# A query stage in less memory, with a fifth context group loaded beside it, in a one-core transformer-block kernel

## What is computed

```
x = x + xattn(layernorm(x), ctx, Wq, bq, Wk, bk, Wv, bv)    # q @ k.T, softmax over 1601, @ v, no scale
x = x + attn(layernorm(x), ...)                             # causal, 16 heads, + exp(denom_bias) in the sum
x = x + ffn(layernorm(x), ...)                              # two mixtures of 64 experts, top 2, gelu between
```

## Time and profile before

| what | value |
|---|---|
| median of 3 runs | 1413.24 us |
| the profiled execution, its own time | 1403.64 us |
| its span, first to last instruction | 1401.8 us |
| PE busy | 1272.8 us, 91% of the span |
| DVE busy | 810.4 us, 58% |
| chain that ended last | PE 75%, DVE 10%, issue 6%, DMA 4% |
| granted TensorE clock, mean | 0.962 |

### The profile page before, as it was taken

The page is one execution under the profiler, slowest core; times in us unless marked ns, Lnnn a source line. Parts: engine busy times, 40 slices in busy tenths (PEclk is TensorE's granted clock), DMA queues, the critical chain, the costliest instruction groups (busy, mean ns, idle before and its releaser), DMA issues.

```text
span 1401.8 us, 61977 instructions
## 1 busy us (share of the span) xinstructions
PE 1272.8 (91%) x27944; PEld 821.5 (59%) x27944; DVE 810.4 (58%) x1511; ACT 442.6 (32%) x927; POOL 207.9 (15%) x364
## 2 busy tenths in 40 slices
PE   7999799999999999999999999578888888798886
PEld 4875233333333335566666666467777777787775
DVE  2435577777767661656556556345473746247666
ACT  0322122122122122222112221136363636336554
POOL 0100000000000000111111111115151523113212
PEclk9999999999999999999999999888999999759999
DMA  8674979989989974311100111212121205522212
GB/s 307 170 226 148 311 250 321 298 278 323 300 278 318 298 252 103 58 60 60 60 37 23 60 45 61 79 43 90 60 109 41 120 0 230 194 90 91 106 45 90
DMA packets 68080, 211.50 MB, mean 151 GB/s; under 512 B 14448, under 2 KB 30832, under 8 KB 53520
## 3 DMA queue, kind: packets, MB, share of 16 engines
q1 hardware_dynamic: 67984, 210.16, 44.5%
HBM read 172.37 MB, written 37.75 MB: 150 GB/s over the span
## 4 chain that ended last, share of the span: by engine, by line
PE 75%; DVE 10%; issue 6%; DMA 4%; ACT 2%; POOL 2%; SPq 1%; DVEq 0%; POOLq 0%; ACTq 0%
PE ps L680 13%; PE ps L529 10%; PE ps L981 8%; PE ps L1756 5%; PE ps L1710 4%; PE ps L233 4%; DVE arena L541 4%; PE ps L437 4%; PE ps L1082 4%; PE ps L1725 3%; PE ps L1742 2%; PE ps L1681 2%; PE ps L670 2%; PE ps L1002 2%; PE ps L1799 2%
## 5 line engine op out<-in xcount | busy, mean ns | idle before, releaser
L541 DVE STREAM_TRANSPOSE arena<-arena 128x448 f32<-128x448 f32 (+1 forms) x512 | 264.2, 577 | 124.7 <-PE ps L529 100.6
L529 PE MATMUL ps<-arena 32*64 32x400 f32 (+1 forms) x4096 | 203.9, 509 | 7.6 <-DVE arena L541 6.9
L680 PE MATMUL ps<-arena 128*64 128x512 f32 x832 | 189.1, 598 | 0.0
L529 PEld LDWEIGHTS ps<-arena 32*64 32x64 f32 x4096 | 75.3, 131 | 104.6 <-DVE arena L541 51.1
L680 PEld LDWEIGHTS ps<-arena 128*64 128x64 f32 x832 | 55.5, 136 | 121.3 <-issue 111.9
L562 ACT ACTIVATE arena<-ps,arena 128x384 f32<-128x384 f32 x64 | 36.4, 583 | 276.3 <-DVE arena L553 276.3
L981 PE MATMUL ps<-arena 128*128 128x256 f32 x512 | 114.8, 382 | 6.4 <-ACT arena L939 6.4
L1596 ACT COPY arena<-ps 128x512 f32<-128x512 f32 x128 | 75.3, 588 | 142.2 <-PE ps L1725 78.5
L981 PEld LDWEIGHTS ps<-arena 128*128 128x128 f32 x512 | 96.0, 190 | 21.2 <-ACT arena L939 7.2
L1416 DVE SCALAR_TENSOR_TENSOR arena<-ps,arena 128x512 f32<-128x512 f32 x64 | 68.8, 1106 | 39.9 <-PE ps L1742 39.6
L1756 PE MATMUL ps<-arena 64*64 64x32 f32 x4096 | 84.5, 236 | 6.5 <-DVE arena L1433 5.8
(11 more groups left out here) (144 smaller groups left out, 1860.3 us busy)
## 6 DMA issues: line engine op xcount, KB each, us to landing
arena<-ctx SPq DMA_DIRECT2D x64, 1024.0 KB
arena<-ctx SPq DMA_DIRECT2D x32, 768.0 KB
arena<-q_n SPq DMA_DIRECT2D x64, 256.0 KB, 11.8
h_n<-arena SPq DMA_DIRECT2D x16, 1024.0 KB, 4.5
arena<-h_n SPq DMA_DIRECT2D x16, 1024.0 KB, 9.8
arena<-x SPq DMA_DIRECT2D x16, 512.0 KB, 4.4
arena<-ctx SPq DMA_DIRECT2D x32, 256.0 KB
x_n<-arena SPq DMA_DIRECT2D x16, 512.0 KB, 3.1
```

Of the source, the lines that this page charges most:

```text
L529: last = pe.matmul(ps[b * SEQ:(b + 1) * SEQ, tb, 0:WIDTH[tb]], qs[p % 2][r, db, b * SEQ:(b + 1) * SEQ], z[r, at % RING, b, 0:WIDTH[tb]], s ...
L541: vec.transpose(z[:, at % RING, :, g * 224:g * 224 + nt * 32].rearrange("p b (j t) -> p b j t", t=32), slots[slot_of(k)][:, :, 0:nt, db * ...
L680: last = pe.matmul(ps[b * SEQ:(b + 1) * SEQ, OB, :], probt[:, j, b * SEQ:(b + 1) * SEQ], slot[:, b, jj, :], start=j == 0, stop=j == TILES - 1)
```

## The change

- `xn` is gone: rows are normalised in place in `xt`. So `load_rows(n)` now waits until tile n-2 has been transposed (`s_t`) and not just normalised.
- The area of slot 2 (group 4) holds only `bq_wide` and `lnt[0]`, both used up early. `xt`, `u_wide` and `parts` move to `spare`; `lnt` of tiles 1 to 7 alternates between two pieces of the zone where wq and wk lay.
- `queries` of tiles 0 to 5 alternate between the two halves of `qs[1]`, the buffer for the queries of odd pairs; tiles 6 and 7 use `xt`. ACT's results of tiles 2 to 5 therefore wait for the store of the tile two before (`s_qd`), and the queries of pair 1 can be loaded only after six stores have landed.
- SP's list is written anew: biases and weights ahead of the first rows, and group 4 in two parts between the stores of tiles 4, 5 and 6. `cross` no longer waits and no longer loads it.
- PE multiplies the first two of the four blocks of wqk before it transposes tile 0.
- POOL's last memset waits for products of tile 6 and not for a store.

```diff
-    queries = [temp(DC, QROWS) for _ in range(4)]
-    queries += [queries[0], queries[1], spare(DC, QROWS), spare(DC, QROWS)]
+    xt = [spare(2 * D) for _ in range(2)]
+    halves_of_qs = qs[1].rearrange("p (u m) q -> p u (m q)", u=2)
+    queries = [t.rearrange("p (c n) -> p c n", c=DC) for t in [halves_of_qs[:, n % 2] for n in range(6)] + xt]
...
+    u_wide = spare(DC, 32)
+    parts = spare(QROWS)
     bq_wide = area(DC, P)
-    xt = [area(2 * D) for _ in range(2)]
-    xn = [area(2 * D) for _ in range(2)]
-    lnt = [area(DC, QROWS) for _ in range(2)]
-    u_wide = area(DC, 32)
-    parts = area(QROWS)
+    own_lnt = [temp(DC, QROWS)]
+    temp.at = temp_at + TILES * P
+    own_lnt.append(temp(DC, QROWS))
+    lnt = [area(DC, QROWS)] + [own_lnt[n % 2] for n in range(1, QUADS)]
...
         def load_rows(n):
             if n >= 2:
-                sp.wait_ge(s_xn, 2 * (n - 2) + 2)
+                sp.wait_ge(s_t, 2 * (n - 2) + 2)
...
-        load_rows(0)
-        load_rows(1)
-        sp.dma_start(wq, a["wq"].rearrange("(c p) d -> p c d", p=P)).then_inc(s_w, 16)
-        sp.dma_start(wk, a["wk"].rearrange("(c p) d -> p c d", p=P)).then_inc(s_w, 16)
         sp.dma_start(bqc, a["bq"]).then_inc(s_b, 16)
         sp.dma_start(bkc, a["bk"]).then_inc(s_b, 16)
+        sp.dma_start(wq, a["wq"].rearrange("(c p) d -> p c d", p=P)).then_inc(s_w, 16)
+        sp.dma_start(wk, a["wk"].rearrange("(c p) d -> p c d", p=P)).then_inc(s_w, 16)
+        load_rows(0)
+        load_rows(1)
         load_context(sp, a, slots, s_c, 0)
-        load_rows(2)
         sp.wait_ge(s_pad, 2)
+        load_rows(2)
         load_context(sp, a, slots, s_c, 1, (0,))
         load_rows(3)
         load_context(sp, a, slots, s_c, 1, (1,))
+        store_queries(0)
         load_rows(4)
-        load_rows(5)
-        store_queries(0)
         load_context(sp, a, slots, s_c, 2, (0,))
-        load_rows(6)
         sp.wait_ge(s_qd, 8 * 16)
         load_queries(sp, a, qs, s_qs, 0)
-        load_queries(sp, a, qs, s_qs, 1)
         store_queries(1)
-        load_rows(7)
+        load_rows(5)
         load_context(sp, a, slots, s_c, 2, (1,))
         store_queries(2)
+        load_rows(6)
         load_context(sp, a, slots, s_c, 3, (0,))
         store_queries(3)
+        load_rows(7)
         load_context(sp, a, slots, s_c, 3, (1,))
-        for n in range(4, QUADS):
-            store_queries(n)
+        store_queries(4)
+        load_context(sp, a, slots, s_c, 4, (0,))
+        store_queries(5)
+        sp.wait_ge(s_qd, 8 * 16 * 6)
+        load_queries(sp, a, qs, s_qs, 1)
+        load_context(sp, a, slots, s_c, 4, (1,))
+        store_queries(6)
+        store_queries(7)
...
-        pool.wait_ge(s_qd, 6 * 8 * 16)
+        pool.wait_ge(s_q, DC * (QUADS - 1))
...
-            if n >= 2:
-                vec.wait_ge(s_t, 2 * (n - 2) + 2)
             for par in range(2):
-                vec.tensor_scalar(xn[u][:, par * D:(par + 1) * D], xt[u][:, par * D:(par + 1) * D],
+                vec.tensor_scalar(xt[u][:, par * D:(par + 1) * D], xt[u][:, par * D:(par + 1) * D],
...
-            if n in (4, 5):
-                act.wait_ge(s_qd, 8 * 16 * (n - 3))
+            if 2 <= n < 6:
+                act.wait_ge(s_qd, 8 * 16 * (n - 1))
...
-        for par in range(2):
-            transposes(0, par)
         pe.wait_ge(s_w, 32)
         pe.wait_ge(s_b, 32)
         for m in range(DC):
+            if m == 2:
+                for par in range(2):
+                    transposes(0, par)
...
-        sp.wait_ge(s_re, 2 * QUADS)
-        load_context(sp, a, slots, s_c, 4)
```

More of the change, by code:

```diff
@@ L284, in store_queries @@
                       .then_inc(s_qd, 16)
+        sp.dma_start(bqc, a["bq"]).then_inc(s_b, 16)
+        sp.dma_start(bkc, a["bk"]).then_inc(s_b, 16)
+        sp.dma_start(wq, a["wq"].rearrange("(c p) d -> p c d", p=P)).then_inc(s_w, 16)
+        sp.dma_start(wk, a["wk"].rearrange("(c p) d -> p c d", p=P)).then_inc(s_w, 16)
         load_rows(0)
         load_rows(1)
-        sp.dma_start(wq, a["wq"].rearrange("(c p) d -> p c d", p=P)).then_inc(s_w, 16)
-        sp.dma_start(wk, a["wk"].rearrange("(c p) d -> p c d", p=P)).then_inc(s_w, 16)
-        sp.dma_start(bqc, a["bq"]).then_inc(s_b, 16)
-        sp.dma_start(bkc, a["bk"]).then_inc(s_b, 16)
         load_context(sp, a, slots, s_c, 0)
+        sp.wait_ge(s_pad, 2)
         load_rows(2)
-        sp.wait_ge(s_pad, 2)
         load_context(sp, a, slots, s_c, 1, (0,))
@@ L384, in transposed @@
                 act.wait_ge(s_q, DC * (n - 1))
-            act.copy(lnt[n % 2][:, :, par::2], ps[:, TB, :].rearrange("p (c n) -> p c n", c=DC)).then_inc(s_te, 1)
+            act.copy(lnt[n][:, :, par::2], ps[:, TB, :].rearrange("p (c n) -> p c n", c=DC)).then_inc(s_te, 1)
         def results(n, h):
             act.wait_ge(s_q, n * DC + 2 * h + 2)
-            if n in (4, 5):
-                act.wait_ge(s_qd, 8 * 16 * (n - 3))
+            if 2 <= n < 6:
+                act.wait_ge(s_qd, 8 * 16 * (n - 1))
             for m in (2 * h, 2 * h + 1):
@@ L426, in transposes @@
             for c in range(DC):
-                last = pe.transpose(ps[:, TB, c * P:(c + 1) * P], xn[n % 2][:, par * D + c * P:par * D + (c + 1) * P], ident)
+                last = pe.transpose(ps[:, TB, c * P:(c + 1) * P], xt[n % 2][:, par * D + c * P:par * D + (c + 1) * P], ident)
             last.then_inc(s_t, 1)
@@ L437, in products @@
                     last = pe.matmul(ps[:, QB + h, m % 2 * QROWS:(m % 2 + 1) * QROWS], wqk[:, c, m * P:(m + 1) * P],
-                                     lnt[n % 2][:, c, :], start=c == 0, stop=c == DC - 1)
+                                     lnt[n][:, c, :], start=c == 0, stop=c == DC - 1)
                 last.then_inc(s_q, 1)
@@ L444, in row_parts @@
             for c in range(DC):
-                last = pe.matmul(ps[c * 32:(c + 1) * 32, RB, 0:QROWS], u_wide[:, c, :], lnt[n % 2][:, c, :],
+                last = pe.matmul(ps[c * 32:(c + 1) * 32, RB, 0:QROWS], u_wide[:, c, :], lnt[n][:, c, :],
                                  start=True, stop=True)
```

## The result

| | before | changed | ratio, 95% interval |
|---|---|---|---|
| first comparison (4 runs each) | 1414.03 us (1409.38 to 1414.88) | 1398.62 us (1395.43 to 1399.88) | 0.9894 (0.9866 to 0.9922) |
| profiled execution | 1403.64 us | 1399.88 us | |
| its span | 1401.8 us | 1398.1 us | |
| its mean granted clock | 0.962 | 0.959 | |

The changed kernel is faster, by 15.4 us in the medians of that comparison, where 8.4 were forecast. But the two profiled executions differ by 3.8 us only.

The account below looks back on a forecast made before the run. PE was taken to bound the first 540 us, with a hole at 150 to 160 us where it waits for context DMA. -9.0 + 0 + 0.6 = -8.4 us took 1413.24 to 1404.8 us, range 1399.5 to 1411.3.

Parts of the forecast that it names:

- The hole: At 150 to 160 us PE waits for context group 5, queued behind group 4; loading group 4 earlier gains 9.0 us.
- rival 2: The hole stays in part: group 5's own last issues leave 2 us of waiting; total about -4.4 us; chance 0.12.
- The start: Weights first bring the first product 2.1 us earlier, tile 0's transposes cost about 1.95; net 0, bounds -0.7 and +0.5.
- rival 3: Without early transposes the first products run slowly for longer: +2.1 us, total -6.3; chance 0.08.
- Tile 5: Its rows of x, issued behind the second store, are normalised at 74.6, PE wants them at 74.06: loss 0.6 us.
- ACT's waits: ACT's results of tile 3 wait for the second store, 1.1 us late, with 3 us of cover left: cost 0.
- Sum -8.4: Hole -9.0, start 0 and tile 5 +0.6 us, taking the median from 1413.24 to 1404.8 us.
- Rivals 1, 4 and 5: 1: tile 5 lands at 75.9, total -3.5, 0.14; 4: late rows, total +4, 0.07; 5: later pair waits, 0.04.
- The range: Whole-kernel time forecast between 1399.5 and 1411.3 us, leaving rivals 4 and 5 outside.
- Numbers: The prediction's part that sets the range from term bounds and run scatter, and gives the forecast 0.55.
- theory B: From the follow-ups: the change brings some 7 us more by moving the last stage against its clock; ratio 0.989.

Follow-up runs that it names:

- before again: The kernel before, run once more unedited against itself: 1406.48 us over 12 runs, ratio 0.9988.
- rows first: Changed kernel with rows of tiles 0 and 1 loaded ahead of weights and biases, tile 0 transposed ahead of the products: 1402.0 us, ratio 0.9938 to the kernel before.

## Why the prediction was right and wrong

**The hole, -9.0: right.** -8.96 by the same matmuls; before again, -8.9. That late group 4 causes it is shown by taking the one change back (8.0 us in that setting). DVE's wait for group 5 is gone, where under 1 us was allowed; rival 2 is out.

**The start, 0: +0.8 in the first trace, +0.6 against rows first,** just outside the bound of +0.5. First product and transposes came within 0.3 us. The rest is how long the first products stay slow. With early transposes they took 5.93, 5.83 and 5.66 us, without 6.66, 5.14, 5.93, 5.78, 5.63 and 5.25: no difference beyond chance, so rival 3 is out, though warming up in earnest does save 3 us.

**Tile 5, +0.6: mis-sized, +1.8.** The landing was forecast to 0.4 us (70.9 against 71.32). The step that failed is the other half of the subtraction, "PE wants it at 74.06". That time was read from a trace with a spell of half clock at 37 us, which had made PE 1.7 us late. The changed kernel's trace has no such spell and is 0.8 us late by its start, so PE came 0.9 us earlier, at 73.1, and had to wait until 74.9. The stretch of 30 to 40 us of the kernel before had a granted clock of 0.85, and I did not read it as a cost that may come or go:

```profile
30.00:40.00 10.00, 9.49 (x44) 6.97 (x44) 3.02 (x9) 0.62 (x1) 0.93 (x2) 0.85 0.00 1
```

Those 1.7 us are the -1.7 of the comparison. Nor is the +1.8 fixed: it was 1.5 to 2.0 in five traces with this order of loads and 0 in two.

**ACT's waits, 0: right**, with 5.22 us of waiting and no cost to PE. One load more would have used the cover up.

**Sum -8.4: right for the mechanism**, -8.05 in the trace and -7.6 to -9.5 over all runs. That the trace met it so closely is luck: the start was 0.8 too small, tile 5 1.2 too small, and the spell's -1.7 stood in no term. Rivals 1, 4 and 5 did not come.

**The range: wrong.** The step that failed is in "Numbers": "less 3.9, the scatter of the three runs downwards". Single executions of this kernel lie between 1398 and 1421 us and follow the granted clock of the last stage, 8.4 us for each 0.01. Three runs showed 5.5 us of that spread of some 23. The offset "9.6 us above" between profiled execution and median was of the same kind and was taken as fixed; for the changed kernel it was -1.3. With medians of four runs drawn from all executions of the two kernels, the difference lies between -17 and +1 us in 95 of 100 draws, and 7 in 100 are at -15 or beyond. So 15.4 us needed no second effect, and theory B is not needed: repeated, the ratio was 0.9944 and 0.9954. (Two sums of "Numbers" are off as well: 1403.5 less 3.9 is 1399.6, and -9.0 with the start's +0.5 and tile 5's 1.8 is -6.7 and not -7.1. Neither would have brought 1398.62 inside.) For the same reason "about 0.5% can be told" was too bold for a few runs. What sets off the spells of half clock behind 870 us in one execution and not in the next stays open.

## What to carry to other kernels

When memory keeps a load out of a phase in which DMA idles, look for the buffers that lie in its place; here two in-place tricks and one shared buffer moved 3.67 MB out of the way of the next loads and removed a hole of 9 us, for about 2 us of tighter waits. Compare traces by the n-th instruction of the bounding engine: it separates what the edit does from what happens later by itself. And before a small forecast, look at the clock: a stretch with a granted clock below 1 is a cost that may be missing in the next execution, and a median of three runs may be off by more than the effect.

## What the runs showed of the hardware that I had not expected

- The first products after an idle start took between 5.14 and 6.66 us for the same eight instructions, and 3.71 when PE had been kept busy with unread transposes from 1.92 us on. In the traces without that and with the one-column products in rows the slow phase ended between 13 and 17 us; with one-column products in between the large ones it reached to 19.4 us.
- Short spells of half clock, 1.7 us each in cost, stood in ten of eleven traces near 23 or 37 us, although PE had no pause over 0.8 us ahead of them. What it had done was rows of 16 one-column products among the large ones; that these are the cause is not shown.
- The last stage ran 27 us at half clock in some executions with PE 26.5 of 27 us busy by the records; the whole time varied by over 20 us with it.
- Three kernels with 36 more PE instructions at their start had a pause of PE of 1.2 to 1.5 us near 573 us, in the middle of 128 like products and ended by nothing that the profile names; the other ten had none there.
